# Summing the states of a scan on TensorE: C spread by DMA, one product a state in SBUF, transposes that accumulate in PSUM

## The reference, cut to what matters

```python
def step(state, inp):
    ut, dtt, bt, ct = inp
    dA = jnp.exp(jnp.clip(dtt[:, :, None] * A, -5.0, 5.0))
    dB = dtt[:, :, None] * bt[:, None, :] * ut[:, :, None]
    state = dA * state + dB + 1e-06
    y = jnp.sum(state * ct[:, None, :], axis=-1) + D * ut
    return (state, y)
# Bm = u @ B_w.T ; Cm = u @ C_w.T : 16 values a token each, the same for all channels
y = y * silu(z);  x = x + y @ out_w.T
```

## Time and profile before

| | |
|---|---|
| median of 3 runs | 1398.56 us (1398.08 to 1398.73) |
| span of the profiled execution | 1397.1 us (what lies around it in the median run: 1.5) |
| instructions | 27129 |
| TensorE busy | 1212.7 us, 87% |
| VectorE busy | 1174.3 us, 84% |
| ScalarE busy | 916.8 us, 66% |
| GpSimd busy | 846.8 us, 61% |
| DMA | 132.29 MB, mean 95 GB/s |

### The profile page before, as it was taken

One profiled execution on the slowest core, in us unless ns is written; L12 is line 12 of the kernel. 1 busy time (PEld: TensorE's weight loads), 2 busy tenths in 40 slices (PEclk: granted clock), 3 DMA queues, 4 the chain that ended last, 5 costly groups with the idle time before them and its releaser, 6 DMA issues.

```text
span 1397.1 us, 27129 instructions
## 1 busy us (share of the span) xinstructions
PE 1212.7 (87%) x8709; PEld 1013.2 (73%) x8709; DVE 1174.3 (84%) x2236; ACT 916.8 (66%) x1464; POOL 846.8 (61%) x1370
## 2 busy tenths in 40 slices
PE   6878897899989898998989899898989989898883
PEld 4556666577877777777777778777877878787773
DVE  1699999998898979998898989989798988998423
ACT  4665666577875766777676777668577768772321
POOL 4445445854366864768656783768647684665554
PEclk9899999999999999999999999999999999999997
DMA  6000000032322343143321433232330333256783
GB/s 179 1 1 9 1 9 6 22 125 61 114 82 64 106 136 103 44 128 99 121 67 34 147 97 98 86 111 81 109 120 29 125 92 121 78 184 190 251 271 85
DMA packets 111646, 132.29 MB, mean 95 GB/s; under 512 B 10128, under 2 KB 82704, under 8 KB 111504
## 3 DMA queue, kind: packets, MB, share of 16 engines
q1 hardware_dynamic: 98416, 111.31, 25.7%
q0 software_dynamic: 8192, 16.79, 4.0%
q10 hardware_dynamic: 4896, 2.43, 0.6%
HBM read 102.37 MB, written 28.11 MB: 93 GB/s over the span
## 4 chain that ended last, share of the span: by engine, by line
PE 35%; DVE 31%; ACT 13%; issue 12%; POOL 5%; DMA 2%; DVEq 0%; POOLq 0%; SPq 0%; ACTq 0%
DVE h L1281 14%; DVE yT L1299 11%; PE p_db L1036 5%; PE p_misc L1060 5%; PE p_hT L1053 5%; PE p_dn L1218 4%; PE p_gu L1206 3%; ACT dA L872 3%; ACT L969 2%; POOL ysel L791 2%; ACT hm L969 2%; PE p_gu L1197 2%; PE p_misc L1097 2%; PE p_misc L1141 1%; PE p_misc L1115 1%
## 5 line engine op out<-in xcount | busy, mean ns | idle before, releaser
L1281 DVE TENSOR_TENSOR_SCAN h<-dA,p_db 128x512 f32<-128x512 f32 x512 | 602.4, 1205 | 86.3 <-PE p_db L1036 85.3
L735 POOL TENSOR_SCALAR dBT<-wT,bcT 128x256 f32<-128x256 f32 x704 | 337.1, 479 | 249.2 <-ACT wT L903 140.1
L1299 DVE SCALAR_TENSOR_TENSOR yT<-p_hT,bcT,yT 128x256 f32<-128x256 f32 x960 | 402.2, 472 | 18.0 <-PE p_hT L1053 17.9
L872 ACT ACTIVATE dA<-dt_sb,A_sb 128x510 f32<-128x510 f32 x512 | 330.6, 710 | 26.6 <-DVE h L1281 25.5
L1036 PE MATMUL p_db<-ident,dBT 128*128 128x128 f32 x2048 | 284.4, 277 | 49.4 <-DVE h L1281 44.0
L1053 PE MATMUL p_hT<-ident,h 128*128 128x128 f32 x2048 | 288.9, 279 | 29.8 <-DVE yT L1299 16.6
L1036 PEld LDWEIGHTS p_db<-ident,dBT 128*128 128x128 f32 x2048 | 233.4, 142 | 96.7 <-issue 84.7
L1053 PEld LDWEIGHTS p_hT<-ident,h 128*128 128x128 f32 x2048 | 233.0, 143 | 74.8 <-issue 42.2
L777 POOL DMA_INDIRECT xs_dram<-xn,slot x128 | 127.0, 992 | 90.0 <-ACT dA L872 38.3
L929 ACT ACTIVATE dBT<-wT,eps,bcT 128x256 f32<-128x256 f32 x320 | 163.9, 593 | 0.0
L791 POOL DMA_INDIRECT ysel<-ys_dram,slot x128 | 123.5, 965 | 57.0 <-issue 33.9
(11 more groups left out here) (189 smaller groups left out, 1533.1 us busy)
## 6 DMA issues: line engine op xcount, KB each, us to landing
wring<-w_moe_dram SPq DMA_DIRECT2D x169, 384.0 KB, 4.3
xt<-xs_dram SPq DMA_DIRECT2D x41, 256.0 KB, 5.7
ys_dram<-yo SPq DMA_DIRECT2D x34, 256.0 KB, 2.3
dA<-w_moe_dram SPq DMA_DIRECT2D x16, 384.0 KB, 5.6
x_sb<-x_dram SPq DMA_DIRECT2D x16, 256.0 KB, 4.5
out_dram<-x SPq DMA_DIRECT2D x15, 256.0 KB, 2.5
xs_dram<-ysel SPq DMA_DIRECT2D x4, 512.0 KB, 6.0
xs_dram<-xn,slot POOLq DMA_INDIRECT x128, 2.3
```

The lines of the kernel that those rows point to most:

```text
L735: op = pool.tensor_scalar(dBT[:, j % DBT_RING, c], wT[:, g % 2, c], bcT[:, g % 2, c, n:n + 1], STATE_EPS, ALU.mult, ALU.add)
L872: act.activation(dst[:, :, 1:], src[:, :, 1:], ACT.Exp, scale=A_sb[:, half, n:n + 1]).then_inc(exp_done, 1)
L1281: dve.tensor_tensor_scan(h[:, j % 2, half], dA[:, j % DA_RING, half], p_db[half][:], 0.0, ALU.mult, ALU.add).then_inc(scan_done, 1)
L1299: op = dve.scalar_tensor_tensor(yT[:, g % 2, cc], p_hT[pair][:, c], bcT[:, g % 2, cc, NS + n:NS + n + 1], yT[:, g % 2, cc], ALU.mult, ALU.add)
```

## The change

C is no longer used by token. The projection still gives B and C by token; ScalarE now stores them apart in `bcT`. A new piece `cT` transposes C (4 chunks of 16 states) on TensorE to 64 rows of 128 tokens, ScalarE copies these to `c_rows`, and SP stores them to a small tensor in DRAM as 16 rows of 512 tokens (`cs`). For each unit SP loads one row, 2 KB, into all 128 partitions of `c_wide`, a ring of 6 slots, three units ahead (`c`). VectorE multiplies both halves of the scanned states by that row in place, one instruction of 1024 elements (`t`, for unit u - 1). TensorE's 8 transposes then accumulate in PSUM over the 16 states of a group (`p_y`, the banks of `p_hT`; `h` is now the transposing of u - 2), and once a group ScalarE copies the two banks to `yT` (`e0`, `e1`). `h` gets three slots, `dA` five for six, `yT` one for two. All fifteen tables of pieces have a new order; the pieces of the experts are the same. In the tail 16 weight tiles for 14 fit in freed buffers. The diff, cut:

```diff
-BY_ACT = 1
-DA_RING = 6
+DA_RING = 5
+H_RING = 3
+C_RING = 6
+C_LEAD = 3
...
 PE_SLOTS = (
-    "U h N G i0 i1 X", "h U yb0 N i0 i1 yb1 G", "X h U xnT i0 i1 N G", "h u0 N U v0 i0 i1 X X",
...
+    "N U h U i0 i1 U G h", "G N yb0 i0 G h X G X", "N i1 yb1 U i0 h xnT U i1", "u0 v0 X i0 i1 X h N U",
...
 DVE_SLOTS = (
-    "stats1 s0 s1 y0 P y1", "C Q s0 s1 Q P yd0 y0", "s0 s1 yd1 y1 Q C y0 y1", "s0 C C y0 s1 P y1 P Q",
...
+    "C C s0 s1 stats1 t s0 P P", "Q s1 Q Q t yd0 Q s0 t", "yd1 s1 C Q s0 s1 t C t", "P P s0 P P s1 x1 t C",
...
 POOL_SLOTS = (
...
+    "c d c S C", "ln1 d c S gate0", "C c gate1 d S", "c d C S d", "c d c c C", "ln2 d C d C", "c S c C C",
+    "d C C d S", "c S C S c", "clip0 w0 d c clip1", "S S d S w1", "C S c S C", "d c S d c", "d C d C C", "S S")
 SP_SLOTS = (
...
+    "W T c Y c c", "c W W c Y W", "c Y T Y W xl", "O c T W T W", "c O O T T O", "T W c T c O", "Y Y Y O Y T",
+    "W c Y W O T", "Y Y c W c Y", "W O T W O T", "cs Y T T O O", "W c O T O W", "W c Y c Y O", "O T Y O")
...
+            def store_rows(g):
+                sp.wait_ge(misc_emptied, misc_at["cT", g])
+                at_least(sp, times_c, NS * (g - 1))
+                sp.dma_start(row_sets[g % 2].rearrange("n (c t) -> c n t", c=CHUNKS), c_rows[:]).then_inc(rows_stored, 16)
+
+            def load_c(j):
...
+                g, n = divmod(j, NS)
+                if n == 0:
+                    sp.wait_ge(rows_stored, 16 * (g + 1))
+                at_least(sp, times_c, j - C_RING + 1)
+                sp.dma_start(c_wide[:, j % C_RING], row_sets[g % 2][n:n + 1].broadcast_to([P, TOK])
+                             ).then_inc(c_loaded[j % C_RING], 16)
...
+            def empty_y(g, pair):
+                act.wait_ge(y_in_psum, PAIRS * (NS * g + NS - 1) + pair + 1)
...
+                act.activation(yT[:, 2 * pair:2 * pair + 2], p_y[pair][:], ACT.Copy).then_inc(y_emptied, 1)
...
-            def states_by_token(j):
+            def sum_states(j):
...
+                pe.wait_ge(times_c, j + 1)
                 for pair in range(PAIRS):
...
+                    if n == 0:
+                        at_least(pe, y_emptied, PAIRS * (g - 1) + pair + 1)
...
+                            mm = pe.matmul(p_y[pair][:, c, half * P:(half + 1) * P],
+                                           h[:, j % H_RING, half, t0:t0 + P], ident[:], is_transpose=True,
+                                           start=n == c == half == 0, stop=n == NS - 1 and c == half == 1,
+                                           skip_group_check=True)
...
             def scan_state(j, half):
...
-                    at_least(dve, hT_in_psum, PAIRS * (j - 1))
+                    at_least(dve, y_in_psum, PAIRS * (j - H_RING + 1))
...
-            def sum_states(j, pair):
+            def multiply_states(j):
...
-                    op = dve.scalar_tensor_tensor(yT[:, g % 2, cc], p_hT[pair][:, c],
-                                                  bcT[:, g % 2, cc, NS + n:NS + n + 1],
-                                                  yT[:, g % 2, cc], ALU.mult, ALU.add)
...
+                dve.wait_ge(scan_done, HALVES * (j + 1))
+                dve.wait_ge(c_loaded[j % C_RING], 16 * (j // C_RING + 1))
+                dve.tensor_tensor(h[:, j % H_RING], h[:, j % H_RING], c_wide[:, j % C_RING].rearrange(
+                    "p (o t) -> p o t", o=1).broadcast_to([P, HALVES, TOK]), ALU.mult).then_inc(times_c, 1)
```

More of the change, by code:

```diff
@@ L335, in routed_quad @@
     return b, at - XT0[b]
[L338 to L345, removed]
 def of_kind(kind, j):
@@ L413, in build @@
         dBT = sb("dBT", [P, DBT_RING, CHUNKS, CH])
-        h = sb("h", [P, 2, HALVES, TOK])
-        yT = sb("yT", [P, 2, CHUNKS, CH])
-        y_more = sb("y_more", [P, CHUNKS, CH]) if BY_ACT > 1 else None
+        h = sb("h", [P, H_RING, HALVES, TOK])
+        c_wide = sb("c_wide", [P, C_RING, TOK])
+        yT = sb("yT", [P, CHUNKS, CH])
         yz = sb("yz", [P, HALVES, TOK])
@@ L460, in build @@
         p_db = [pb(f"p_db{i}", [P, TOK]) for i in range(HALVES)]
-        p_hT = [pb(f"p_hT{i}", [P, 2, CH]) for i in range(PAIRS)]
+        p_y = [pb(f"p_y{i}", [P, 2, CH]) for i in range(PAIRS)]
         p_gu = [pb(f"p_gu{i}", [P, 2, 2 * P]) for i in range(2)]
@@ L479, in build @@
         spare = [part[:, n * WROW:(n + 1) * WROW] for part, most in (
-            (dA[:].rearrange("p n h t -> p (n h t)"), 8), (dBT[:].rearrange("p n c d -> p (n c d)"), DBT_RING * CHUNKS * CH // WROW),
-            (dt_sb[:].rearrange("p n h t -> p (n h t)"), 2)) for n in range(most)]
+            (dA[:].rearrange("p n h t -> p (n h t)"), places_in(DA_RING, HALVES * TOK)),
+            (dBT[:].rearrange("p n c d -> p (n c d)"), places_in(DBT_RING, CHUNKS * CH)),
+            (dt_sb[:].rearrange("p n h t -> p (n h t)"), places_in(2, HALVES * TOK)),
+            (c_wide[:].rearrange("p n t -> p (n t)"), places_in(C_RING, TOK))) for n in range(most)]
         def weights_of(at):
@@ L491, in weights_of @@
             return wring[:, place], w_loaded[place], 16 * (len(range(place, TAIL_TILE, W_RING)) + turn + 1)
-        gu_banks = [p_gu, [p_db[i][:].rearrange("p (f t) -> p f t", f=2) for i in range(2)], p_hT]
+        gu_banks = [p_gu, [p_db[i][:].rearrange("p (f t) -> p f t", f=2) for i in range(2)], p_y]
         hm_of = [hm[:]] + [wT[:, j].rearrange("p (i f) t -> p i f t", f=2) for j in range(2)]
@@ L530, in build @@
         scan_done = sem("scan_done")
[L531 to L534, removed]
+        rows_stored = sem("rows_stored")
+        c_loaded = [sem(f"c_loaded{j}") for j in range(C_RING)]
+        times_c = sem("times_c")
+        y_in_psum = sem("y_in_psum")
+        y_emptied = sem("y_emptied")
         yz_ready = sem("yz_ready")
@@ L646, in _ @@
                         load_x(k)
+                    if name == "cs" and group_of(k, 1) is not None:
+                        store_rows(k + 1)
+                    if name == "c":
+                        load_c(u + C_LEAD)
                     if name == "T":
@@ L994, in _ @@
                         state_input(u + DB_LEAD)
-                    if name in ("m0", "m1") and u - NS * k < BY_ACT:
-                        multiply_state(group_of(k, 0), u - NS * k, int(name[1]))
+                    if name in ("e0", "e1") and group_of(k, -1) is not None:
+                        empty_y(k - 1, int(name[1]))
                     if name in MISC_STAGE and group_of(k, MISC_STAGE[name]) is not None:
@@ L1052, in states_by_token @@
                             t0 = (2 * pair + c) * P
-                            mm = pe.transpose(p_hT[pair][:, c, half * P:(half + 1) * P],
-                                              h[:, j % 2, half, t0:t0 + P], ident[:])
-                    mm.then_inc(hT_in_psum, 1)
+                            mm = pe.matmul(p_y[pair][:, c, half * P:(half + 1) * P],
+                                           h[:, j % H_RING, half, t0:t0 + P], ident[:], is_transpose=True,
+                                           start=n == c == half == 0, stop=n == NS - 1 and c == half == 1,
+                                           skip_group_check=True)
+                    mm.then_inc(y_in_psum, 1)
             def convolve(g, half, part):
@@ L1143, in use_misc @@
                                            start=q == 0, stop=q == HALVES - 1)
+                if name == "cT":
+                    pe.wait_ge(misc_emptied, misc_at["bc", g])
+                    mm = pe.transpose(bank[0:CHUNKS * NS, 0:P], bcT[:, g % 2, 1].rearrange("p c n -> p (c n)"), ident[:])
                 if name in ("z0", "z1"):
@@ L1222, in down @@
                     mm.then_inc(down_in_psum, 1)
-            begun = None
+            begun = set()
             for k in STEPS:
@@ L1234, in _ @@
                     if name in MISC_REST.values():
-                        begun = name
+                        begun.add(name)
                     if name in MISC_REST:
-                        assert begun == MISC_REST[name]
-                        begun = None
+                        begun.remove(MISC_REST[name])
                     if name in MISC_REST and group_of(k, 1) is not None:
@@ L1531 @@
                for name in ("xs0", "xs1", "ys0", "ys1")]
+    scratch += [nc.dram_tensor(f"{name}_dram", (NS, TOK), F32, kind="Internal").ap() for name in ("rows0", "rows1")]
     build(nc, *args, *scratch, out)
```

122 lines of the change are left out of this document (46 added, 76 removed), and 47 rows, old and new, of tables (ACT_FIRST, ACT_SLOTS, DVE_FIRST, DVE_LAST).

## The result

The changed kernel takes 1377.13 us (median of 4 runs, 1375.66 to 1378.04) against 1398.64: a ratio of 0.9839, 95% interval 0.9825 to 0.9853. It is faster by 21.5 us where 48 were forecast. The profiled execution spans 1375.8 us.

The account below looks back on a forecast made before the run. Neither TensorE nor VectorE alone was taken to bind the middle, each held by the other part of the time; VectorE bound the early stage. Middle -36, early -9, last groups -4, end +1: -48, forecast 1350 us, range 1325 to 1375.

Parts of the forecast that it names:

- the start: Before 213.83 us, where VectorE binds: -4.1 us for each of 2.2 groups, -9; first C row 0 (0 to 5).
- the middle: Twelve groups from 213.83 to about 1175 us: period from 80.5 to 77.5 us, -36 in all.
- the last group: Last two groups, VectorE 94% busy for some 1.5 of them: -4 us.
- the tail: After the last scan, a product and two copies replace multiply-adds: +1 us.
- the product's price: VectorE's 16 products a middle group: 1.19 us each, plus 0.17 waiting for GpSimd's current instruction.
- the price of the lock for GpSimd: VectorE instructions with two SBUF inputs also stop GpSimd's SBUF reads: +8.9 us a group, 3.7 more with indirect DMAs.
- the 4.2 us a group in which TensorE waits for others: Middle groups: TensorE's waits for ScalarE, GpSimd and small gaps, taken to stay beside 73.1 us of work.
- the second rival: TensorE saturates: new order also takes most of the other 4.2 us, period 74.5, total 1312 us; chance 0.20.
- Rival 1: GpSimd becomes the bound: products stop it too, its need 82.5 us a middle group, total 1415; chance 0.18.
- the old loop: Scan, transposes, multiply-add, next transposes: gone with the new order, and with it 7.1 us of TensorE's waits.
- C loads free: One 256 KB load a state, issued some three states ahead, taken as hidden: 0.
- Exponentials' shorter ring: `dA` with five slots: ScalarE's exponentials wait for the scan of the state before; 0, upper end 1 us a group.

Follow-up runs that it names:

- e1: Changed kernel with VectorE's product replaced by an instruction over the same 1024 elements with one SBUF input, multiplication by C left out; 1306.0 us, ratio 0.9316.
- e9: e1 with three of the four `dBT` instructions of a state on GpSimd cut in two halves each; 1364.0 us, ratio 0.9750.
- e4: Changed kernel with all five engine orders behind the last group taken from the kernel before; 1366.5 us, ratio 0.9762.
- e7: Changed kernel with the scan writing over `p_db` in PSUM and each half multiplied from there, whole computation; 1401.5 us, ratio 1.0023.

## Why the prediction was wrong

The gain fell 27 us short. By the marks of the table above: the start gave 10 us more than forecast, the middle 14 less, the last group 9 less and the tail 13 less.

- *Direction and the product's price: right.* The product was put at 1.19 us and 0.17 of waiting; 1.20 and 0.15 were measured, together 1.35 against 1.36. That the waiting happens at all was read from the rows before the change, and it is so. VectorE's busy time fell by 2.3 us a middle group for 3.5.
- *The step that failed: the price of the lock for GpSimd was left out of the sum and kept as a rival.* Its size there was right (8.9 + 3.7 = 12.6 us a group against 11.0 measured, scatters and gathers among them), and e1 shows what the lock as a whole costs, VectorE's waits among it: 5.6 us a middle group, of which e9 puts most on GpSimd's side. The argument against it, that GpSimd's length "is the same throughout", was empty: before the change the longest kind of VectorE instruction with two SBUF inputs took 0.35 us in the mean.
- *A second term hid the first: the 4.2 us a group in which TensorE waits for others were taken to stay.* Without the lock they go nearly all: e1 runs at 72.4 us a group, less than the 73.0 that TensorE's busy time was taken to need, where 77.5 was forecast and even the second rival said 74.5. So the change was worth -7.5 us a group and the lock took 5.6 back: -1.9 measured, -3.0 forecast. That the middle missed by only 14 us is luck: the two errors have opposite signs. TensorE's waits for VectorE, taken as gone with the old loop, are 32.6 us in ten groups for 39.7 before and 21.8 in e1.
- *Rival 1 was right in mechanism, wrong in price:* it added the lock to the full wait for `wT`, but that wait shrank (48.1 us in six groups, 34.7 in ten), so that the need of 82.5 us that it came to was never reached. The sign that it named, `dBT` near 0.7 us, came out between the two, at 0.61.
- *The start:* -18.6 up to group 3 for -9. VectorE's relief of 4.1 us a group was sized right (12.0 in three groups), counted for 2.2 groups only, and the 7 us of VectorE's idle time that the first group lost were not in the sum.
- *The tail, +14.4 for +1, and the last group, +5.2 for -4.* A step of the sum failed here as well, and in the net it weighs more (23 us) than the middle (14 us): it priced the pieces from group 15 on and not the order in which the queues take them. In the tail it isn't the lock: e1's is 126.7 us. For the last scan to the end e4 gives 9 of the 14 back by orders alone; of the other 5 the cause is open. In the last group VectorE's busy time fell from 73.8 to 68.7 us and the group got longer all the same; e1 needs 83.9 us for it, so the lock can be some 2.6 of the 5.2, and the rest is open. The lower granted clock in both is untested.
- *C loads free, transposes at the same price:* right. *Exponentials' shorter ring:* put at 0; ScalarE's wait for scans rose from 25.5 to 58.4 us over the span (50.0 in e1), and no run shows whether it costs time.

## What to carry to other kernels

Before moving an operation of VectorE to two SBUF inputs, count what GpSimd does on SBUF beside it: each such instruction can stop GpSimd for nearly its whole length (here 0.66 us of GpSimd's time in the mean for a product of 1.20), and an engine that looked 67% busy may have no slack at the places where others wait for it. Price a mechanism whose first half is in the rows in the sum, not among the rivals. Where all queues are reordered, follow the one chain behind the last piece of the main loop through every queue, for it has nothing to hide under.

## What the runs showed that was not expected

- TensorE's busy time for the same work is no constant: 73.2 us a group before, 72.2 after, 70.7 in e1, for 538 matmuls each time. Where it waits less, its records cover less. "Busy 91%" before the change was an upper bound of its need.
- VectorE doesn't always get in at the next end of a GpSimd instruction. At 633.29 it stood through two in a row, and the longest product, 3753 ns, waited some 2.5 us.
- A scan in place in PSUM takes 1218 ns for 1206 with its output in SBUF (e7).
